# Second attention: the row maximum ahead of the split of the exponentials in VectorE's program

## The reference

```
q = jnp.einsum('nd,hdk->hnk', node_matrix, Wqs)
k = jnp.einsum('nd,hdk->hnk', node_matrix, Wks)
v = jnp.einsum('nd,hdk->hnk', node_matrix, Wvs)
scores = jnp.einsum('hqk,hmk->hqm', q, k) * kd ** (-0.5)
scores = scores + IDENTITY_BIAS * eye - MASK_VAL * (1.0 - adj)
att = jax.nn.softmax(scores, axis=-1)
return jnp.einsum('hqm,hmk,hko->qo', att, v, Wo)
...
x = _layernorm(x + _L0_gnn_ref(...), axis=-1)
x = _layernorm(x + _L1_gnn_ref(...), axis=-1)
```

## Time and profile before

| | |
|---|---|
| time of the kernel, median of 3 runs | 4451.31 us (4447.39 to 4452.5) |
| time of the profiled execution | 4445.76 us |
| span of the profiled execution | 4444.0 us |
| busy over the span: PE, PEld, DVE, ACT, POOL | 3814.1, 2541.4, 3499.3, 3344.7, 356.3 us |
| granted TensorE clock, mean over the span | 0.934 |

### The profile page before, as it was taken

One profiled execution on the slowest core, in us unless ns is written; L12 is line 12 of the kernel. 1 busy time (PEld: TensorE's weight loads), 2 busy tenths in 40 slices (PEclk: granted clock), 3 DMA queues, 4 the chain that ended last, 5 costly groups with the idle time before them and its releaser, 6 DMA issues. The chain is left out here.

```text
span 4444.0 us, 104687 instructions
## 1 busy us (share of the span) xinstructions
PE 3814.1 (86%) x42884; PEld 2541.4 (57%) x42884; DVE 3499.3 (79%) x6000; ACT 3344.7 (75%) x4172; POOL 356.3 (8%) x559
## 2 busy tenths in 40 slices
PE   7942327999999996992999999999999999999977
PEld 4422227999999993440555555555555555555533
DVE  2155558999999997763888898898889888888734
ACT  1124438999999992220999999999999999999942
POOL 0000000000000000002011120111212011020000
PEclk9965558999999997995999999999999999999999
DMA  2089996555555446765344353544535444353133
GB/s 71 38 275 359 351 342 211 191 183 189 184 184 179 166 150 188 237 208 161 84 124 115 101 143 91 136 113 104 135 100 138 100 119 125 87 155 96 49 107 132
DMA packets 399302, 691.07 MB, mean 156 GB/s; under 512 B 79784, under 2 KB 272488, under 8 KB 361832
## 3 DMA queue, kind: packets, MB, share of 16 engines
q1 hardware_dynamic: 339040, 608.86, 46.0%
q0 software_dynamic: 16512, 58.73, 4.1%
q10 hardware_dynamic: 43280, 16.92, 1.4%
HBM read 532.82 MB, written 151.59 MB: 154 GB/s over the span
## 5 line engine op out<-in xcount | busy, mean ns | idle before, releaser
L1214 DVE CUSTOM_DVE_ANT_0 m_junk<-m_rough,m_rows 128x1024 bf16<-128x1024 f32 x1024 | 1253.3, 1224 | 286.5 <-PE m_rough L1081 225.2
L1163 ACT ACTIVATE m_scores<-m_strip 128x1024 f32<-128x1024 fp8e4 x1024 | 1052.3, 1028 | 102.2 <-POOL m_strip L1012 37.7
L1177 ACT ACTIVATE m_whole<-m_scores 128x1024 int32<-128x1024 f32 x1024 | 1037.9, 1014 | 33.2 <-PE m_scores L1114 22.9
L614 PE MATMUL g_acc<-g_vals,g_pos 128*128 128x130 f16 x8192 | 955.9, 218 | 51.1 <-DVE g_neg L569 51.1
L531 ACT ACTIVATE g_step<-g_arow,k_steep 128x512 fp8e4<-128x512 f32 x1536 | 948.4, 707 | 40.2 <-DVE g_pos L562 37.2
L614 PE MATMUL g_acc<-g_vals,g_neg 128*128 128x130 f16 x8192 | 955.4, 221 | 0.0
L1095 PE MATMUL m_acc<-m_v,m_halves 128*128 128x129 f16 (+1 forms) x16384 | 896.1, 208 | 45.2 <-ACT m_got L1140 45.2
L1095 PEld LDWEIGHTS m_acc<-m_v,m_halves 128*128 128x128 f16 x16384 | 750.1, 98 | 279.5 <-issue 185.9
L614 PEld LDWEIGHTS g_acc<-g_vals,g_pos 128*128 128x128 fp8e4 x8192 | 801.8, 98 | 62.0 <-DVE g_neg L569 37.1
L1109 PE MATMUL m_scores<-m_qA,m_kA 128*128 128x512 f16 x2048 | 780.8, 381 | 5.8 <-ACT m_scores L1163 5.7
L614 PEld LDWEIGHTS g_acc<-g_vals,g_neg 128*128 128x128 fp8e4 x8192 | 784.5, 96 | 0.0
(11 more groups left out here) (153 smaller groups left out, 3089.2 us busy)
## 6 DMA issues: line engine op xcount, KB each, us to landing
g_vals<-scr_gat_v SPq DMA_DIRECT2D x128, 1040.0 KB, 5.2
m_v<-scr_v SPq DMA_DIRECT2D x64, 1032.0 KB, 7.7
b_stage<-in_adj SPq DMA_DIRECT2D x64, 1024.0 KB, 9.2
m_kA<-scr_k_hi SPq DMA_DIRECT2D x128, 512.0 KB, 6.1
scr_row_mask<-b_rowm SPq DMA_DIRECT2D x64, 512.0 KB, 8.6
m_kB<-scr_k_lo SPq DMA_DIRECT2D x64, 512.0 KB, 5.4
m_rows<-scr_row_mask POOLq DMA_DIRECT2D x64, 512.0 KB, 7.3
scr_gat_v<-b_tab SPq DMA_DIRECT2D x32, 520.0 KB, 9.8
```

The source lines that it names most:

```text
L614: mm = pe.matmul(acc[:, b, it, lo:hi], edges[:, n % RING, t, rows], vals[:, b, 4 * j + t, lo:hi], start=j == 0 and t == 0 and lo == 0, sto ...
L1163: nc.scalar.activation(scores[:, n % 2], strip[:, 2 * st:2 * st + 2, :].rearrange("p t i -> p (t i)"), ACT.Copy, bias=-BIG, scale=BIG / ED ...
L1177: nc.scalar.activation(whole[:, st % 2], scores[:, st % 2], ACT.Exp, scale=0.125).then_inc(exped, 1)
L1214: nc.vector.tensor_tensor_reduce(out=junk[:, n % 2], in0=rough[:].rearrange("p a m -> p (a m)"), in1=rows[:, n % TC, n // TC * WIDE:(n // ...
```

## The change

In VectorE's list for step g the maximum of tile g + 28 stood behind the split of step g - 1; now it stands ahead of it. `reduce_max` moves with the maximum, `divide` stays behind the split, `make_offset` stays last. Nothing is added or taken out, and the lists of the other engines are what they were.

```
             for g in range(U * STEPS):
                 u, st, m = g // STEPS, g % STEPS, g + EARLY
+                if m % TILES == 0 and m <= U * TILES:
+                    reduce_max(m // TILES - 1)
+                if m < U * TILES:
+                    take_max(m)
                 if g > 0:
                     split_up((g - 1) // STEPS, (g - 1) % STEPS, g - 1 < STEPS)
-                if m % TILES == 0 and m <= U * TILES:
-                    reduce_max(m // TILES - 1)
                 if st == 8 and u > 0:
                     divide(u - 1)
-                if m < U * TILES:
-                    take_max(m)
                 if m % TILES == 0 and m <= U * TILES:
                     make_offset(m // TILES - 1)
             split_up(U - 1, STEPS - 1)
```

## The result

The changed kernel takes 4487.29 us in the median (4481.02 to 4492.14), the kernel before 4449.8 beside it: ratio 1.0083, 95% interval 1.0066 to 1.0101, 37 us more. Its profiled execution took 4481.02 us over a span of 4479.2 us, 35.2 us more than that of before.

What follows compares the result with a forecast made beforehand. PE and ACT were taken to be in balance at about 2.02 us a step, with PE waiting 0.70 a unit for the copy. 62 x 0.355 = 22 us on a median of 4451.3 gave 4473 us, 8-in-10 range 4456 to 4487.

Steps and rivals of the forecast that it cites:

- likeliest case: Whole kernel: the forecast slowdown with what shifts it, long splits included, 15.5 to 28 us plus 2 of scatter; chance 0.79.
- What bounds: In attend: PE and ACT in balance, 2.02 us a step, and PE idle 0.70 a unit waiting for copy_out.
- Maxima, split's own waits: VectorE's list: maxima run at their old times, and splits one step later still have room; cost 0 for each.
- The exponential of step 2: Unit's step 2: exponential waits for the older split, 0.36 late; seed, copy and products follow, 0.355 in 62 units, 22 us.
- The ordinary steps: Steps without the copy: exponential 0.29 late, hidden by room before the scores that need its seed; cost 0.
- The cover: Room between a seed's end and its scores: 0.48 less 0.14, some 0.3 us, less up to 0.1 over a unit.
- every step pays: Rival: dependency loop from maximum through split, exponential, seed and scores sets the pace beyond 0.34 more; 31 us, 4504; chance 0.06.
- The rest of the list: Division, offset and their stores: the division's 0.15 a unit stays, one tile further on; offset and stores cost 0.
- The page on the shared ports: VectorE against GpSimd: later join could stretch one split a unit by 0.34, costing 2 to 9 us more, 4475 to 4482.
- B: Theory tested after the measurement: the long split that GpSimd stretches in step 3, 1.19 us, is what costs the time.
- Nothing to be seen: Rival: the exponential's slip does not reach PE; median stays at 4451, or within 9 us; chance 0.11.
- Faster: Rival: maxima have less ahead of them, PE's 0.15 at each division goes, 9.5 us gained, 4442; chance 0.04.

Runs made afterwards that it cites:

- both terms undone: Changed order with a third buffer for the exponentials and mask-row waits only in the first unit of a chunk: 4450.39 us, ratio 0.9998 to the kernel before.

## Why the prediction was right, and where it was off

*The number.* The direction and the way were right, the size was too small. The forecast was 4473, the median 4487.29: 14 above it, outside the likeliest case's own 4465 to 4482, and 0.3 above the upper end of 4456 to 4487. That the whole range reached so far is partly luck: its upper end was there for long splits, which came and cost nothing. What filled the distance were a lag and a division, 3 and 6 us, that the sum had too low, the clock in unit 63 (1.4), and some us that no trace places.

*What bounds.* Right. PE's beat of 2.02 and the one wait a unit for the copy carried the case.

*Maxima, split's own waits.* Right: ordinary steps stay at 2.02, and with both terms undone the stage is back within 0.3 us. The cost of 0 for the maxima did not hold for the one behind the division, see below.

*The exponential of step 2.* The mechanism was right, link by link, and the one buffer more removed it. Its size was off in one term: the lag from the split's end to the exponential's start, which I took as 0.04 from the first attention, is 0.09 here. 0.31 + 0.09 = 0.40, and PE's wait 1.11, not 1.06. In 62 units that is 25 us, not 22.

*The ordinary steps.* The cover held, but it was thinner than I wrote. I had the exponentials 0.29 late; from step 5 on they are 0.45 to 0.6 late. My sign "0.04 behind the end of a split in most steps" did not come: in the median only those of steps 1, 2, 5 and 10 start at the end of a split, 0.09 behind it. Behind the copy they are held by the split that follows the maximum of step 4, and again in step 10 by the one behind the division, and in between ScalarE's own beat of 2.03 gives nothing back. In step 8 of the changed kernel the seed ends at 3046.56 + 1.03 = 3047.59, and the scores that need it start at 3047.90: 0.31 left, where I had written 0.48 less up to 0.1. In the median over units 1 to 61 most steps from step 7 to the next unit's step 0 have 0.24 to 0.38 left, against some 0.8 before. I had also taken PE's lag behind ACT from the copy, 0.14; its scores start 0.06 behind a seed that they wait for (new order with the copy first: the seed ends at 3017.07 + 1.05 = 3018.12, the scores start at 3018.18). So the ring of the rival "every step pays" did not close, with steps at 2.02, but it came near: in units 40, 42, 57 and 59 scores of a few steps start 0.05 to 0.1 behind the end of their seed. The two rows of step 8 are these, and the two exponentials that are held.

```profile
3046.56 1.03 ACT L1163 ACTIVATE m_scores<-m_strip 128x1024 f32<-128x1024 fp8e4 x1
...
3047.90 0.38 PE L1109 MATMUL m_scores<-m_qA,m_kA 128*128 128x512 f16 x1
```

```profile
3039.38 1.02 ACT L1177 ACTIVATE m_whole<-m_scores 128x1024 int32<-128x1024 f32 x1 [0.38 <-DVE m_halves L1239]
...
3049.75 1.03 ACT L1177 ACTIVATE m_whole<-m_scores 128x1024 int32<-128x1024 f32 x1 [0.16 <-DVE m_halves L1239]
```

*The rest of the list.* This step failed: "so the 0.15 stays, one tile further on". It became 0.24. I had costed the division as the same work in a same gap and had not asked what else the gap holds: the two waits for the mask rows ahead of every fourth maximum, which the division had covered. I had even seen that starts of the maxima move "by up to 0.1 from step to step", and used it only to lower the estimate. 6 us.

*The page on the shared ports.* The stretch did come, and longer than I allowed: splits of step 2 last 1.19 in the median of the units where they lasted 0.69. In the changed kernel:

```profile
3035.21 0.74 POOL L1027 TENSOR_TENSOR m_num<-m_got 128x256 f32<-128x256 f32 x1
3035.31 0.08 DVE L1214 DVE_READ_ACCUMULATOR2_ANT m_most<- 128x1 f32 x1
3035.31 1.19 DVE L1239 TENSOR_SCALAR m_halves<-m_whole 128x2048 f16<-128x2048 uint16 x1
```

GpSimd's addition starts 0.10 ahead of the split and ends at 3035.95, the split ends 0.55 behind that. The Trainium skill, "SBUF — State Buffer", section "Who interferes with whom", says that a fast-mode operation which finds the shared ports taken by GpSimd blocks fully. The trace agrees in that the split outlasts the addition; since 0.55 is less than a split's 0.69, it does not show that all of the split's work waited. It cost nothing: the exponential that needs this split starts at 3036.85, 0.10 behind the max tile of 3036.75, as in the kernel before. In the median over the units this distance is 0.10 in both kernels. The maximum behind the stretched split is not held either: the split ends at 3036.50, before the max tile that this maximum waits for even starts (3036.75). So B falls.

*Rivals and size.* "Nothing to be seen" and "Faster" did not come. The 37 us are, by the traces, 25.7 and 6.5 in the two places, 0.7 in the other steps of units 1 to 61, 1.4 at the lower clock in unit 63, and some 3 outside the stage, which I cannot place. The stages ahead of `attend`, in which nothing differs, end at different times in different executions (first copy from 2142.4 to 2153.1 us over these traces), so single executions differ by some us and the stage is the better measure, though one trace against one is good to some 2 us only.

## What to carry to other kernels

When two entries of an engine's list are swapped, look at the consumer's *buffer* wait and not only at its data wait: the data came no later here, but the buffer was freed a step later. Then ask what stands behind the delayed instruction in its own engine's list. 0.4 us of lateness in most steps was free until it met the one instruction for which the bounding engine already waited, and there it counted in full. And when a one-off piece of work is moved to "the same gap, one further on", list the waits of both gaps: what it used to hide comes out.

## What the runs showed of the hardware

An instruction of VectorE with two more semaphore waits, all passed long before, started 0.09 later behind the matmul that released it than without them (0.69 against 0.60). ScalarE started 0.09 behind the end of VectorE's split, and 0.04 behind VectorE's operation in the first attention; I don't know why these differ. TensorE started 0.06 behind the end of a seed and 0.14 behind that of the copy. A split of 0.69 us lasted 1.19 when it began 0.10 behind a GpSimd addition of 0.74, and 0.78 when it began 0.51 behind it (new order with the third buffer). In unit 63 the granted clock fell to its lower level for some 3 us after 1.84 us of idle time of TensorE in the changed kernel's trace (0.58 in the mean of 4266 to 4270 us), and stayed at the higher one after the same idle time in that of before.
